# Joins between the layers of a four-layer kernel: when semaphores are cleared, what each layer's start waits for, and how the result is stored

## The reference, cut to what matters

```python
x = L0(x, ctx)      # grouped-query attention over 1500 context rows, then layer norm (32 batches of 56 rows, 256 wide)
x = L1(x, state)    # RWKV block: token shift, five mixes, a scan over 56 steps, group norm, feed-forward part
# L2: the rows x are latents, ctx is the context
q = latents @ q_w + q_b;  kv = concat([ctx, latents]) @ kv_w + kv_b
attn = softmax(where(mask, q k^T / 16, -inf)) @ v
attn_out = attn @ out_w + out_b + latents
out = gelu(rmsnorm(attn_out) * w @ mlp_w1 + b1) @ mlp_w2 + mlp_b2
x = out + latents
x = L3(x, state)    # RWKV block like L1, with its own weights
```

## Time and profile before

| | us |
|---|---|
| median of 3 runs | 3312.01 (3310.67 to 3313.16) |
| the profiled execution | 3310.44 |
| its span, from first to last instruction | 3308.6 |

### The profile page before, as it was taken

One profiled execution on the slowest core, in us unless ns is written; L12 is line 12 of the kernel. 1 busy time (PEld: TensorE's weight loads), 2 busy tenths in 40 slices (PEclk: granted clock), 3 DMA queues, 4 the chain that ended last, 5 costly groups with the idle time before them and its releaser, 6 DMA issues. The chain is left out here.

```text
span 3308.6 us, 63547 instructions
## 1 busy us (share of the span) xinstructions
PE 2864.8 (87%) x18753; PEld 1516.3 (46%) x18753; DVE 2017.9 (61%) x4196; ACT 1415.6 (43%) x3023; POOL 652.9 (20%) x482
## 2 busy tenths in 40 slices
PE   5799999999999999999768887599999987788885
PEld 3344444444444444444334444356666655444442
DVE  4667676777677677677367887244444441168774
ACT  2255555555555555555513221254444443221221
POOL 5221222122112212221023332000000000033331
PEclk7699999999999999999979998699999998899996
DMA  6333433343243334333010000111110100100000
GB/s 198 102 89 105 119 108 83 111 116 104 81 120 107 106 88 120 107 98 78 15 62 0 1 0 0 47 34 33 27 33 27 33 15 28 59 0 0 1 0 23
DMA packets 117152, 205.18 MB, mean 62 GB/s; under 512 B 39681, under 2 KB 84463, under 8 KB 116463
## 3 DMA queue, kind: packets, MB, share of 16 engines
q1 hardware_dynamic: 116846, 201.08, 21.3%
HBM read 156.09 MB, written 44.59 MB: 61 GB/s over the span
## 5 line engine op out<-in xcount | busy, mean ns | idle before, releaser
L589 DVE CUSTOM_DVE_ANT_0 masked<-ps_a,mask 112x750 f32<-112x750 f32 x1024 | 941.9, 936 | 378.5 <-PE ps_a L476 369.6
L549 ACT ACTIVATE probs<-ps_a 128x448 f32<-128x448 f32 (+1 forms) x1536 | 743.3, 542 | 547.4 <-PE ps_a L442 543.5
L476 PE MATMUL ps_a<-ks,q_row 96*112 96x375 bf16 x2048 | 529.6, 342 | 57.5 <-DVE part_max L589 34.8
L442 PE MATMUL ps_a<-q_sc,ks 99*128 99x448 bf16 (+1 forms) x1536 | 450.3, 359 | 50.3 <-ACT probs L549 28.5
L462 PE MATMUL ps_a<-probs,vp 128*32 128x224 f32 x6144 | 380.5, 366 | 1.2 <-ACT probs L549 0.9
L476 PEld LDWEIGHTS ps_a<-ks,q_row 96*112 96x112 bf16 x2048 | 220.4, 133 | 330.0 <-issue 271.7
L2014 DVE CUSTOM_DVE_ANT_0 f_masked<-ps_c,f_mp 112x432 f32<-112x432 f32 x256 | 145.6, 606 | 218.2 <-PE ps_c L1866 218.2
L442 PEld LDWEIGHTS ps_a<-q_sc,ks 99*128 99x128 bf16 (+1 forms) x1536 | 132.7, 100 | 283.2 <-issue 234.9
L239 POOL CAST k_piece<-kv_t 64x1500 bf16<-64x1500 f32 x32 | 45.6, 1426 | 1043.3 <-ACT kv_t L231 1043.1
L462 PEld LDWEIGHTS ps_a<-probs,vp 128*32 128x32 f32 x6144 | 164.8, 111 | 158.7 <-ACT probs L549 59.1
L218 PE MATMUL ps_a<-ctx_t,wkv 128*128 128x375 f32 x512 | 197.7, 512 | 20.5 <-DVE x_nat L350 10.8
(11 more groups left out here) (283 smaller groups left out, 3977.9 us busy)
## 6 DMA issues: line engine op xcount, KB each, us to landing
ctx_t<-in_ctx_t SPq DMA_DIRECT2D x32, 1500.0 KB, 8.9
ks<-k_scr SPq DMA_DIRECT2D x64, 562.5 KB, 5.1
mask<-in_mask SPq DMA_DIRECT2D x64, 328.1 KB, 5.4
k_scr<-k_piece SPq DMA_DIRECT2D x64, 281.2 KB, 6.6
k_scr<-k_piece SPq DMA_DIRECT2D x64, 187.5 KB, 6.8
f_context<-in_ctx_t SPq DMA_DIRECT2D x32, 375.0 KB, 3.1
k_scr<-k_piece SPq DMA_DIRECT2D x64, 93.8 KB, 7.1
q_row<-q_scr SPq DMA_DIRECT2D x64, 84.0 KB, 4.5
```

Source lines behind the costliest of these rows:

```text
L442: mm = pe.matmul(out, ks[par][:, j, at], q_sc[par][:, j], start=True, stop=not with_mask)
L476: mm = pe.matmul(ps[0:2 * L, bank + i, 0:SC], q_row[which][:, j, h, gp * 2 * L:(gp + 1) * 2 * L], ks[which][0:SROWS, j, at], start=True, s ...
L549: act.activation(probs[t % 2][0:n, i], ps[0:n, k % SCORE_BANKS, 0:PW] .rearrange("p (h n) -> p h n", h=2), ACT.Exp).then_inc(probs_done, 1)
L589: dve.tensor_tensor_reduce(out=masked[:, u % 2], in0=two_banks(bank, 2 * L), in1=in_two(mask[which][:, c * SU:(c + 1) * SU]), scale=1.0, s ...
```

## The change

1. `clear` is no block any more: a list of instructions in GpSimd's stream. Layer0's semaphores are cleared by rwkv b's GpSimd after its memsets, b's by latent_attention's early block, that stage's by mlp's GpSimd, mlp's by rwkv d's. Rwkv d's own are cleared in a last block, after the result is stored. The semaphores live until their clearing stage is done.
2. rwkv: w1, w2, dw1, dw2 get a semaphore of their own, and the first lora waits for these four alone; "key" waits for the others, whose order begins with wk, wv. GpSimd doesn't wait for loads.
3. rwkv d: SP stores each chunk of x_nat in two DMAs of 224 KB as soon as x2 counts it, and waits for all eight at the end. The store block is gone.
4. latent_attention, early block: ident, mask, query weights, transposed mask and out_b come first, each with its semaphore. TensorE waits only for ident, turns x_nat, then `active`, and makes the queries after Vector's first reduction over that transpose; Vector makes the flags first and y_nat after them.
5. last_quarter stands ahead of every_quarter, and its SP doesn't wait for the memsets.
6. mlp: the bias sum over x_nat is GpSimd's, after the loads; Vector waits for it only after the first four tiles are scaled.

```diff
-def clear(nc, sems):
-    with nc.Block() as block:
-        @block.gpsimd
-        def _(pool):
-            for s in sems:
-                pool.sem_clear(s)
+def clear(pool, sems):
+    for s in sems:
+        pool.sem_clear(s)
...
@@ rwkv
+        mix_loads = [(w1, tag + "w1"), (w2, tag + "w2"), (dw1, tag + "dw1"), (dw2, tag + "dw2")]
+        loads = [(wk, tag + "wk"), (wv, tag + "wv"), (wr, tag + "wr"), (wg, tag + "wg"),
...
                 for dst, name in loads:
                     sp.dma_start(dst[:], a[name]).then_inc(s["loaded"], 16)
                 sp.wait_ge(s["loaded"], 16 * len(loads))
+                if out is not None:
+                    rows = out.rearrange("(g r) l e -> r l g e", r=2)
+                    for c in range(CHUNKS_R):
+                        sp.wait_ge(s["x2"], 2 * (c + 1))
+                        for par in range(2):
+                            pairs = slice(c * CP, (c + 1) * CP)
+                            sp.dma_start(rows[par][:, pairs], x_nat[HALF * par:HALF * par + L, pairs])\
+                              .then_inc(s["stored"], 16)
+                    sp.wait_ge(s["stored"], 16 * 2 * CHUNKS_R)
...
                             if c == 0 and i == 0:
-                                pe.wait_ge(s["loaded"], 16 * len(loads))
+                                pe.wait_ge(s["mix_loaded"], 16 * len(mix_loads))
...
+                            if name == "key" and c == 0 and i == 0:
+                                pe.wait_ge(s["loaded"], 16 * len(loads))
...
-                pool.wait_ge(s["loaded"], 16 * len(loads))
+                clear(pool, old)
...
@@ last_quarter
                 with sp.If(path_of(sp, 1)):
-                    sp.wait_ge(preset, PRESETS)
...
@@ latent_attention
+                    sp.dma_start(ident[:], a["ident"]).then_inc(ident_in, 16)
+                    sp.dma_start(mask_i[:], a["mask_q"]).then_inc(mask_in, 16)
+                    sp.dma_start(q_w[:], a["c_q_w"]).then_inc(q_in, 16)
+                    sp.dma_start(q_b[:], a["c_q_b"]).then_inc(q_in, 16)
+                    sp.dma_start(mask_ti[:], a["mask_t"]).then_inc(mask_t_in, 16)
+                    sp.dma_start(out_b[:], a["c_out_b"]).then_inc(out_b_in, 16)
...
+                @block.gpsimd
+                def _(pool):
+                    clear(pool, old)
...
-                    pe.wait_ge(loaded, 16 * len(loads))
+                    pe.wait_ge(ident_in, 16)
...
+                    pe.wait_ge(act_row, 1)
+                    pe.wait_ge(copied, 1)
+                    pe.transpose(ps[0:1, 0, 0:P], active[:], ident[:]).then_inc(act_t, 1)
+                    pe.wait_ge(q_in, 32)
+                    pe.wait_ge(fl, 2)
                     for n, (c, m) in enumerate(UNITS):
...
-                    pe.wait_ge(act_row, 1)
-                    pe.wait_ge(kept, 1)
-                    pe.transpose(ps[0:1, 0, 0:P], active[:], ident[:]).then_inc(act_t, 1)
...
+        last_quarter(nc, y_nat, a, passed, (ident, kv_w, kv_b, qt, x_t, q_sel, v_b, out_w2, ps), path_of, mp_scr, sems, held)
         every_quarter(nc, y_nat, a, passed, (ident, identb, kv_w, kv_b, qt, x_t, out_w, head_scale, odd_mask, bias_t, ps),
-                      path_of, mb_scr, sems, ctx)
-        last_quarter(nc, y_nat, a, passed, (ident, kv_w, kv_b, qt, x_t, q_sel, v_b, out_w2, ps), path_of, mp_scr, sems, ctx)
-        clear(nc, sems)
+                      path_of, mb_scr, sems, held)
+    return sems
...
@@ mlp
                 pool.memset(eps[:], RMS_EPS).then_inc(preset, 1)
+                pool.wait_ge(loaded, 16 * len(loads))
+                pool.tensor_tensor(x_nat[:], x_nat[:], b2[:].unsqueeze(1).to_broadcast([P, PAIRS, E]),
+                                   ALU.add).then_inc(based, 1)
+                clear(pool, old)
...
-                dve.wait_ge(loaded, 16 * len(loads))
-                dve.tensor_tensor(x_nat[:], x_nat[:], b2[:].unsqueeze(1).to_broadcast([P, PAIRS, E]),
-                                  ALU.add).then_inc(based, 1)
                 dve.wait_ge(rms_set, 1)
                 dve.reciprocal(rrms[:], rms[:]).then_inc(rrms_set, 1)
                 dve.wait_ge(rrms_set, 1)
-                dve.wait_ge(based, 1)
...
                     normalise(0, g)
+                dve.wait_ge(based, 1)
...
@@ program
+        used_d = rwkv(nc, x_nat, a, "d", False, passed, h_d, used_m, out)
+        h_m.close()
         with nc.Block() as block:
-            @block.sync
-            def _(sp):
-                for par in range(2):
-                    sp.dma_start(out.rearrange("(g r) l e -> r l g e", r=2)[par],
-                                 x_nat[HALF * par:HALF * par + L]).then_inc(stored, 16)
-                sp.wait_ge(stored, 32)
+            @block.gpsimd
+            def _(pool):
+                clear(pool, used_d)
```

More of the change, by code:

```diff
@@ L748, in product_order, with rwkv @@
     return out
-def rwkv(nc, x_nat, a, tag, after_layer0, passed):
+def rwkv(nc, x_nat, a, tag, after_layer0, passed, held, old, out=None):
     sems = []
@@ L2097, in _, with latent_attention @@
                     all_bodies(pool, pool_body)
-def latent_attention(nc, x_nat, y_nat, a, passed):
+def latent_attention(nc, x_nat, y_nat, a, passed, held, old, old_held):
     mb_scr = nc.dram_tensor("mb_scr", [B, NQ, SQ], F32).ap()
@@ L2138, in latent_attention @@
         ps = ctx.enter_context(nc.psum_tensor("ps_c", [P, 8, 512], F32))
[L2139 to L2142, removed]
+        loads = [(kv_w, "c_kv_w"), (kv_b, "c_kv_b"), (out_w, "c_out_w"), (head_scale, "head_scale"),
+                 (odd_mask, "odd_mask"), (q_sel, "q_sel"), (v_b, "c_v_b"), (out_w2, "c_out_w2")]
         with ExitStack() as early:
+            ident_in, mask_in, mask_t_in, q_in, out_b_in = [
+                sem("0_" + n) for n in "ident_in mask_in mask_t_in q_in out_b_in".split()]
             loaded, turned, copied, made, kept, neg, act_row, act_t, fl, bt, yb, mb_out = [
@@ L2205, in _ @@
                     dve.tensor_reduce(active[:], mask_a[:], AX_X, ALU.max).then_inc(act_row, 1)
-                    dve.tensor_scalar(bias_t[:], mask_ti[:], 0.0, MASKED, ALU.is_equal, ALU.mult).then_inc(bt, 1)
-                    dve.tensor_tensor(y_nat[:], x_nat[:], out_b[:].unsqueeze(1).to_broadcast([P, PAIRS, E]),
-                                      ALU.add).then_inc(yb, 1)
+                    dve.tensor_scalar(mask_b[:], mask_i[:], 0.0, MASKED, ALU.is_equal, ALU.mult).then_inc(neg, 1)
+                    dve.tensor_scalar(mask_p[:], mask_i[:], 0.0, -MASKED, ALU.is_equal, ALU.mult).then_inc(neg, 1)
+                    dve.wait_ge(ident_in, 16)
+                    dve.tensor_copy(identb[:], ident[:]).then_inc(bt, 1)
                     dve.wait_ge(act_t, 1)
@@ L2217, in _, with mlp @@
                     dve.tensor_copy(flags[:], path[:]).then_inc(fl, 1)
+                    dve.wait_ge(mask_t_in, 16)
+                    dve.tensor_scalar(bias_t[:], mask_ti[:], 0.0, MASKED, ALU.is_equal, ALU.mult).then_inc(bt, 1)
+                    dve.wait_ge(out_b_in, 16)
+                    dve.tensor_tensor(y_nat[:], x_nat[:], out_b[:].unsqueeze(1).to_broadcast([P, PAIRS, E]),
+                                      ALU.add).then_inc(yb, 1)
+        old_held.close()
         def path_of(eng, i):
             return eng.value_load(flags[0:1, i:i + 1], min_val=0, max_val=1)
+        last_quarter(nc, y_nat, a, passed, (ident, kv_w, kv_b, qt, x_t, q_sel, v_b, out_w2, ps), path_of, mp_scr, sems, held)
         every_quarter(nc, y_nat, a, passed, (ident, identb, kv_w, kv_b, qt, x_t, out_w, head_scale, odd_mask, bias_t, ps),
-                      path_of, mb_scr, sems, ctx)
-        last_quarter(nc, y_nat, a, passed, (ident, kv_w, kv_b, qt, x_t, q_sel, v_b, out_w2, ps), path_of, mp_scr, sems, ctx)
-        clear(nc, sems)
-def mlp(nc, x_nat, y_nat, a):
+                      path_of, mb_scr, sems, held)
+    return sems
+def mlp(nc, x_nat, y_nat, a, held, old):
     GM = 4
@@ L2468, in program @@
 def program(nc, a, out):
[L2469 to L2484 removed]
+    with nc.sbuf_tensor("x_nat", [P, PAIRS, E], F32) as x_nat, nc.semaphore("passed") as passed, \
+            ExitStack() as h_a, ExitStack() as h_b, ExitStack() as h_c, ExitStack() as h_m, ExitStack() as h_d:
+        used_a = layer0(nc, x_nat, a, passed, h_a)
+        used_b = rwkv(nc, x_nat, a, "b", True, passed, h_b, used_a)
+        h_a.close()
+        with nc.sbuf_tensor("y_nat", [P, PAIRS, E], F32) as y_nat:
+            used_c = latent_attention(nc, x_nat, y_nat, a, passed, h_c, used_b, h_b)
+            used_m = mlp(nc, x_nat, y_nat, a, h_m, used_c)
+            h_c.close()
+        used_d = rwkv(nc, x_nat, a, "d", False, passed, h_d, used_m, out)
+        h_m.close()
+        with nc.Block() as block:
+            @block.gpsimd
+            def _(pool):
+                clear(pool, used_d)
 def kernel(**inputs):
```

31 lines of the change are left out of this document (11 added, 20 removed).

## The result

The changed kernel takes 3270.1 us, median of 4 executions (3266.8 to 3273.3), against 3311.3 of the kernel before on the same chip: a ratio of 0.988, 95% interval 0.987 to 0.990. In two later series, eight more executions, the medians were 3274.9 and 3273.3, and all twelve lie between 3266.8 and 3283.4. The forecast was 3280.2 within 3270 to 3288, 31.8 less than before. The medians are 41.2 less in the first series and 36.4 and 36.9 less in the later ones: the sign is right and the size roughly so. The first median lies 0.1 inside the range's lower end, where the rival for mlp stood (3271.4). The profiled execution took 3270.4, its span 3268.5, which is 40.1 less than before.

The account below looks back on a forecast made before the run. It took TensorE as the bound within stages and all-engine standstills at joins as full cost; terms -3.6 -5.8 -9.7 -6.2 +0 +4.0 -1.1 -1.9 -7.5 sum to -31.8, giving median 3280.2 us, range 3270 to 3288.

Parts of the forecast that it names:

- the rival for mlp: In mlp the engines don't block each other, or Vector's four tiles go first: -4.8 instead of +4.0, 3271.4 us; chance 0.15.
- Parts 1 and 3: Clears leave the joins, gaining 3.6, 5.8 and 1.1 us; last_quarter's first load issues once the flag is read, gaining 6.2.
- Part 2: Early block of latent_attention: TensorE waits only for ident, transposes keep 5.27 us, 30.25 becomes 20.55; gain 9.7, 9 to 10.7.
- Part 4: The jump around every_quarter, moved behind last_quarter, still costs 4.8 us and eats the clears' 4.8: 0, bounds -3.6 to +1.7.
- The rival "cheap in its new place": The jump behind last_quarter is cheap because engines that finish early could be ahead: 3276.6 us; chance 0.08.
- Part 5: Start of mlp: GpSimd's sum takes 8.8 us and blocks Vector's remaining tiles, +4.0 us, bounds -4.8 and +5.
- one of the prediction's own signs that it is wrong: In mlp one `normalise` should take about 9 us beside GpSimd's sum; staying at 0.35 would show the forecast wrong.
- The weights 0.58 and 0.15: Chances given to the main forecast, 3280.2 us, and to mlp's tiles not being blocked, 3271.4 us.
- the second rival: The clears hid fetching of the next stage's code at the joins before b, c and d; priced at 5, 3285 us; chance 0.13.
- Part 6: rwkv d: lora no longer waits 2.5 us for the last load; gain 1.9, between 1.5 and 2.5; none in b.
- Part 7: Program's end, from x_nat's last write: 17.8 us becomes 10.3 with early stores; gain 7.5, bounds 6 and 8.2.
- The rival on the slower side: Slower than before: 77 us of last_quarter's 580 us loop at 1.2 GHz lose the gain; 80 us give 3320; chance 0.03.

Follow-up runs that it names:

- e5_clear_blocks: The changed kernel with the clears of the four inner joins back in blocks of their own; its execution took 3291.2 us.
- e4_jump_first: The changed kernel with every_quarter ahead of last_quarter again; TensorE starts on f_context 4.85 us later, the join before mlp falls from 7.02 to 0.27.
- e2_sum_first: The changed kernel with b2 loaded first on its own semaphore and GpSimd's sum waiting for it and the root; the execution took 3283.4 us.
- e9: The changed kernel once more, unaltered: median 3273.3 us, ratio 0.988; its profiled execution took 3278.6 us.
- e6_all_loads: The changed kernel with rwkv's first lora waiting for all 17 loads again; in d TensorE starts 16.94 us after the first DMA instead of 13.60.
- e3_sum_vector: The changed kernel with mlp's bias sum back on Vector, ahead of the reciprocal; the execution took 3269.5 us.
- e1_tiles_first: The changed kernel with GpSimd's sum in mlp also waiting for Vector's four normalised tiles; median 3268.6 us.

## Why the prediction came out as it did

**Parts 1 and 3** held: 3.6, 5.7 and 1.1 for the clears, which e5_clear_blocks shows by itself. For the start of last_quarter the table has 6.2, but by the prediction's own cut, from the end of the early block (2107.3), TensorE starts 4.6 later instead of the forecast 4.3, a gain of 5.8.

**Part 2** gave 8.6 for 9.7 by the prediction's cut (30.25 to 21.64), 8.3 by the table's. The step that was mis-sized is the transposes' 5.27, kept "because TensorE starts at 1.2 GHz as now". It does, but the clock stays there for longer. Granted clock of the stretches (before, after, e5_clear_blocks; busy time of PE, PEld, DVE, ACT, POOL, then clock, DMA share, GB/s):

```profile
2107.60:2110.60 3.00, 3.00 (x14) 3.00 (x15) 2.97 (x7) 1.23 (x3) 0.00 (x0) 0.50 0.37 131
2110.60:2112.60 2.00, 2.00 (x20) 2.00 (x19) 2.00 (x1) 1.84 (x5) 0.00 (x0) 0.94 0.00 0
```
```profile
2087.38:2092.38 5.00, 5.00 (x24) 5.00 (x25) 1.56 (x5) 2.61 (x5) 0.00 (x0) 0.50 0.90 271
2092.38:2093.88 1.50, 1.45 (x11) 1.15 (x9) 0.01 (x1) 1.19 (x4) 0.00 (x0) 0.86 1.03 207
```
```profile
2096.37:2099.37 3.00, 3.00 (x14) 3.00 (x15) 1.56 (x5) 1.23 (x3) 0.00 (x0) 0.50 0.82 253
2099.37:2101.37 2.00, 2.00 (x20) 2.00 (x19) 0.00 (x0) 1.91 (x5) 0.00 (x0) 0.97 1.03 300
```

From the means, with 0.50 for 1.2 GHz: the clock is full 3.2 us after the first transpose before, 5.4 after (0.86 over 1.5 us is 0.72 of them at full clock, from 2092.8 on), 3.1 with the clear block. It rose 2.2 later than before, where the bound allowed for 1. That is the whole miss of 1.1: the transposes took 6.34 for 5.27. In the other nine profiles without a clear block there the clock rises 4.9 to 5.6 us after the first transpose. Why it does so isn't shown.

**Part 4** came out just beyond its bound: +1.9 for 0 (bounds -3.6 to +1.7). The step that failed is that the jump costs the same wherever it stands. 2702.8 to 2708.9 are 6.1 us against 4.8, since the branch took 4.72 and not 3.57; the other 0.6 passes before the jump, between y_nat's last write (2701.97) and the block's end. e4_jump_first shows that it is the place: 3.40 at the front, 4.72 at the back. The rival "cheap in its new place" is out, and so is the 108 ns that the Trainium skill (Advanced Engine Details and Errata, section Control Flow Timing) gives for a compare-and-branch: this one took 4720 ns. What no run here shows is why the branch takes these times. The Trainium skill (Runtime: NRT & Kernel Launch, section Instruction fetch mechanics) says that a taken branch to a target outside the window already fetched waits until the page there has been fetched; durations in microseconds agree with that, and the difference between the two places isn't explained by it.

**Part 5** came out on the other side in the first profile: -4.9 for +4.0, and there `normalise` stayed at 0.35, one of the prediction's own signs that it is wrong. The mechanism stands. A Vector instruction stood still for as long as GpSimd's sum ran (8.66 of 8.80 in e2_sum_first), the sum takes 8.8 to 9.0, and where it gets in, the tiles end 3.7 later than before the change (e5, e9; forecast 4.0). What failed is one number: "the loads are there at 2739.86", 8.75 after mlp's start, taken over from the kernel before. In the changed kernel they are there at 9.3 to 9.5: one of SP's issues, that of m_w, takes 1.3 to 1.4 us, and the last load is issued 0.9 later than before (3.3 after the start against 2.4). In the kernel before, that issue was (timeline)

```profile
2731.51 0.43 SPq L2266 DMA_DIRECT2D m_w<-in_mlp_w  x1
```

The delay moves the sum from 0.1 after the first tile's start to within a tenth of a microsecond of the fourth's, and the prediction said "only one tile fits in that time". The weights 0.58 and 0.15 were far too sharp for an order decided by less than one issue's length. What makes the issue slow isn't settled. It appears in every kernel that enters mlp without a clear block (1.28 to 1.76, on m_w or m_ident; 1.07 and 1.11, on m_b or m_w, where the jump stands first) and in neither with one (before and e5: none over 0.6). In this small sense the second rival is right: without the clear blocks 0.9 us of SP's and 1.1 of TensorE's came up that had not been there. That these are a fetching of code, as the rival has it, no run shows.

**Part 6**: lora starts 2.5 earlier and its eight matmuls take 5.41 instead of 4.80, 1.9 in sum, as forecast:

```profile
2856.45 5.41 PE L877 MATMUL ps_d<-d_xx,d_w 128*128 128x448 f32 x8 [3.51 <-DVE d_xx L1138]
```

The wait was read rightly. The 0.6 that the prediction took off, because the clock rises later after an earlier start, came out right by luck. e6_all_loads starts late as before and takes 5.46; and of the ten profiles that start 13.6 to 13.8 after the first DMA, the shortest and the longest are

```profile
2853.57 4.75 PE L877 MATMUL ps_d<-d_xx,d_w 128*128 128x448 f32 x8 [3.51 <-DVE d_xx L1138]
```
```profile
2850.93 6.31 PE L877 MATMUL ps_d<-d_xx,d_w 128*128 128x448 f32 x8 [3.52 <-DVE d_xx L1138]
```

(e3_sum_vector and e4_jump_first). The rest before them is the same, 3.5 us, and the granted clock is 0.50 for the first 3.0 us in the one and the first 6.2 in the other (a mean of 0.99 in the fourth microsecond of the one, 0.90 in the seventh of the other). So the start to the first mix differs between executions by as much as this term (19.0 to 20.6 after the first DMA; 21.6 before the change), and what sets it isn't shown.

**Part 7** gave 8.4 for 7.5, just beyond its bound of 8.2. The mis-sized term is the store: from x_nat's last write to the first clear are 3.75 us, where the prediction had 0.5 + 3.3 + 0.5 = 4.3. The clears with their ends gave the other 0.4: 5.6 for 5.8 + 0.2, though there are 83 and not 81.

**The rival on the slower side** did not occur. last_quarter's loop took 590.0 against 589.5, its clock at full from 2144 on (the same columns as above):

```profile
2144.00:2240.00 96.00, 92.18 (x772) 57.93 (x770) 46.34 (x131) 48.34 (x126) 6.28 (x16) 1.00 0.11 31
```

## What to carry to other kernels

Work between two stages in which every engine stands still was worth its full length here, and could be read off a timeline to a tenth. What follows it was not untouched: TensorE's first 32 transposes and one DMA issue took 1 us longer each. If a change lets two engines that exclude each other start within a microsecond, don't forecast which goes first: give both orders their time, and fix the order in the kernel by a wait, as e1_tiles_first does at no cost that its stages show (the rest of mlp took 124.0 us against 123.8). A jump over code that isn't run cost microseconds at both places where it was measured, and not the same at each: measure it where it will stand. And one profile of a short stretch after a standstill doesn't show what its start costs: the same eight matmuls took 4.75 to 6.31 us.

## What the hardware showed that was not expected

- A taken branch of TensorE over the same code took 3.40 to 3.68 us at one place of the program (three profiles) and 4.72 to 5.21 at another (nine).
- TensorE's clock stayed at 1.2 GHz for 4.9 to 5.6 us of unbroken transposes after 4.2 to 4.5 us of idleness (ten profiles), and for 3.1 to 3.2 after 10 and 20 us of it (one profile each). At lora in rwkv d equal rests of 3.5 us gave anything from 3.0 to 6.2 us.
- Two starts 0.09 us apart (GpSimd's wait ended at 9.37 or 9.46) decide over 8.5 us until the fourth tile and 7.6 of the stage.
- Semaphore clears came 0.065 to 0.072 us apart in GpSimd's stream and 0.12 in TensorE's.
- One DMA issue on SP takes 1.1 to 1.8 us where its neighbours take 0.43, in every kernel without a clear block before mlp.
